# A feed-forward's down product with the weights held still and the activations moving

## The reference

```python
gate_scores = xf @ gate_w.T                 # two experts, top 1
one_hot = one_hot(argmax(softmax(gate_scores)), 2)
masked = xf[None] * one_hot.T[:, :, None]
h = relu(einsum('end,edh->enh', masked, w1) + b1[:, None, :])
expert_out = einsum('enh,ehd->end', h, w2) + b2[:, None, :]
shared = relu(xf @ sw1 + sb1) @ sw2 + sb2
out = expert_out.sum(axis=0) + shared       # then x = layernorm(x + out)
```

## Time and profile before

| | |
|---|---|
| Median of 3 runs | 635.62 us (633.32 to 635.85) |
| Profiled execution, its own time | 635.56 us |
| Its span, first to last instruction | 633.7 us (1.86 us lie around it) |
| `feed_forward0` on PE | 206.08 to 299.09 us |
| Mean granted clock of PE | 0.955 of full speed |

### The profile page before, as it was taken

How to read it: one execution, slowest core, us unless ns; L and a number is a source line. 1 busy time by engine, 2 the same in 40 slices (tenths; PEclk the granted TensorE clock), 3 DMA queues, 4 the chain that set the end, 5 groups by cost and what they waited for, 6 DMA issues and landing times.

```text
span 633.7 us, 11896 instructions
## 1 busy us (share of the span) xinstructions
PE 576.3 (91%) x4428; PEld 447.1 (71%) x4428; DVE 404.8 (64%) x1057; ACT 266.4 (42%) x531; POOL 226.7 (36%) x327
## 2 busy tenths in 40 slices
PE   3899999999987799999789999999889999999994
PEld 3657667766756599899556666665558888888883
DVE  2477877787764733554657788877246666666655
ACT  3586755575630322220055555555632222222220
POOL 2264545554320535363735555554510000000000
PEclk9699999999978999999959999999869999999999
DMA  5953131223000600002221221220000000000000
GB/s 208 324 197 122 69 134 67 102 100 125 10 1 0 252 1 1 1 2 68 70 74 49 63 63 48 68 73 4 4 1 0 2 1 18 1 18 2 1 18 17
DMA packets 25352, 37.64 MB, mean 59 GB/s; under 512 B 3536, under 2 KB 15568, under 8 KB 24912
## 3 DMA queue, kind: packets, MB, share of 16 engines
q1 hardware_dynamic: 25296, 36.89, 17.5%
HBM read 10.01 MB, written 1.05 MB: 17 GB/s over the span
## 4 chain that ended last, share of the span: by engine, by line
PE 63%; DVE 18%; issue 8%; ACT 3%; POOL 3%; DMA 2%; SPq 2%; POOLq 0%; DVEq 0%; ACTq 0%
PE f_O L1611 7%; PE f_O L801 6%; PE f_H L59 5%; PE f_H L61 5%; PE f_H L60 5%; PE a_MI L485 5%; DVE a_UA L366 4%; PE a_S L1328 4%; PE a_Y L437 4%; PE a_YP L1357 3%; PE a_S L1336 3%; PE a_PJ L59 2%; DVE a_m L1172 2%; PE a_S L423 2%; DVE a_rr L357 2%
## 5 line engine op out<-in xcount | busy, mean ns | idle before, releaser
L226 POOL TENSOR_TENSOR a_Y<-a_Y 128x256 f32<-128x256 f32 x64 | 59.5, 933 | 97.0 <-ACT a_Y L265 97.0
L366 DVE SCALAR_TENSOR_TENSOR a_UA<-a_UA,a_mask 128x768 f32<-128x768 f32 x64 | 68.3, 1075 | 27.1 <-ACT a_UA L273 26.6
L1172 DVE TENSOR_REDUCE a_m<-a_S 128x3 f32<-128x384 f32 x117 | 63.7, 554 | 31.6 <-PE a_S L1336 26.5
L1479 ACT ACTIVATE f_sg<-f_H 128x512 f32<-128x512 f32 x64 | 38.2, 597 | 103.1 <-PE f_H L61 103.1
L1557 DVE TENSOR_TENSOR f_hid<-f_H,f_sg 128x512 f32<-128x512 f32 x64 | 44.3, 692 | 53.2 <-PE f_H L61 43.1
L273 ACT ACTIVATE a_UA<-a_S,a_one 128x768 f32<-128x768 f32 x64 | 57.6, 900 | 44.8 <-PE a_S L424 44.6
L1096 POOL TENSOR_SCALAR_AFFINE_SELECT f_w<-f_w 128x256 f32<-128x256 f32 x128 | 51.8, 407 | 67.9 <-ACT f_w L1143 67.7
L1143 ACT ACTIVATE f_w<-a_ST 128x384 f32<-128x384 f32 x118 | 56.9, 493 | 39.7 <-PE a_ST L1334 39.7
L1611 PEld LDWEIGHTS f_O<-f_w,f_hid 128*128 128x128 f32 x512 | 65.9, 191 | 8.1 <-issue 3.3
L1611 PE MATMUL f_O<-f_w,f_hid 128*128 128x128 f32 x512 | 67.8, 276 | 2.0 <-DVE f_acc L1535 2.0
L437 PE MATMUL a_Y<-a_UA,a_V 128*64 128x256 f32 (+1 forms) x512 | 58.4, 351 | 0.0
(11 more groups left out here) (282 smaller groups left out, 1390.0 us busy)
## 6 DMA issues: line engine op xcount, KB each, us to landing
a_q<-a_c_h SPq DMA_DIRECT2D x16, 256.0 KB, 2.5
a_q<-a_c_l SPq DMA_DIRECT2D x16, 256.0 KB, 2.6
a_k<-a_c_h SPq DMA_DIRECT2D x16, 256.0 KB, 2.5
a_k<-a_c_l SPq DMA_DIRECT2D x16, 256.0 KB, 2.6
f_w<-in_f_w SPq DMA_DIRECT2D x1, 2048.0 KB, 8.8
a_q<-a_c_h SPq DMA_DIRECT2D x16, 128.0 KB
a_q<-a_c_l SPq DMA_DIRECT2D x16, 128.0 KB
a_k<-a_c_h SPq DMA_DIRECT2D x16, 128.0 KB
```

The source lines that it names most:

```text
L226: pool.tensor_tensor(Y2[:, v % 2, j, :], Y[:, v % 2, j, :], Y[:, v % 2, j, :], ALU.mult).then_inc(y2_ready, 1)
L366: dve.scalar_tensor_tensor(UA[:, j % 4, :, :], UA[:, j % 4, :, :], 1.0, mask[:, None, :].to_broadcast([P, 2, SW]), ALU.add, ALU.mult).then ...
L1172: dve.tensor_reduce(m3[:, b % 2, h % H1, :], s_bank(h)[:, 0:SW].rearrange("p (a n) -> p a n", a=3), AX.X, ALU.max).then_inc(max_done, 1)
```

## The change

Down now keeps a 128x128 chunk of w2 stationary and moves all 512 tokens of the block, so the result has features on partitions (`oT`) and must be turned back. Down of chunk n runs three steps (LAG) after its up, within the same block; the last three come after all up steps. Even chunks are one plain F32 product of 512 columns. For odd chunks DVE makes a high and a low F32R part with two instructions, and PE makes three F32R products. DVE writes max(h, -b) in place of relu(h + b); the difference is a constant vector w2'b, made once by PE (`cv_ready`) and added by ACT when it copies `O` to `oT` (`turn`). PE turns `oT` with four transposes into `T[1]`, and the residual reads it there. w2 is split by DVE at the start.

```diff
+    LAG = 3
-        hid = sb("f0_hid", [P, 2, NC, BT])
+        hid = sb("f0_hid", [P, 3, BT])
+        act_h, act_l = sb("f0_act_h", [P, 3, BT], F32R), sb("f0_act_l", [P, 3, BT], F32R)
+        w2_h, w2_l = sb("f0_w2_h", [P, NC, D], F32R), sb("f0_w2_l", [P, NC, D], F32R)
+        neg_b = sb("f0_negb", [P, NC])
...
         def _(act):
+            def turn(i):
+                act.wait_ge(d_ready, (i + 1) * NC)
+                if i >= 1:
+                    act.wait_ge(o_ready, i)
+                act.activation(oT[:, :], O[i % 2][:, :], ACT.Identity, bias=c_vec[:, 0:1]).then_inc(oT_ready, 1)
+
+            act.wait_ge(cv_ready, 1)
+            act.activation(c_vec[:, :], G[:, 64:65], ACT.Copy).then_inc(cv_read, 1)
+            act.wait_ge(cv_read, 1)
             for i in range(NBLK):
                 for c in range(0, NC, 2):
+                    n = i * NC + c
+                    if i >= 1 and c == 4:
+                        turn(i - 1)
+                    act.wait_ge(h_ready, n + 1)
+                    if n >= 6:
+                        act.wait_ge(d_ready, n - 5)
+                    act.activation(hid[:, n // 2 % 3, :], HP[n % 3][:, :], ACT.Relu, bias=b1[:, c:c + 1]).then_inc(h_act, 1)
...
             for t in range(2):
                 prep_high(act, mem, 1, t)
+            turn(NBLK - 1)
...
         def _(dve):
             dve.wait_ge(*before)
+            dve.tensor_scalar(neg_b[:, :], b1[:, :], -1.0, None, ALU.mult)
+            dve.tensor_copy(w2_h[:, :, :], w2[:, :, :]).then_inc(w2_split, 1)
+            dve.wait_ge(w2_split, 1)
+
+            def split_low(third):
+                cs = slice(4 * third, 4 * third + 4)
+                dve.tensor_tensor(w2_l[:, cs, :], w2[:, cs, :], w2_h[:, cs, :].bitcast(F32), ALU.subtract).then_inc(w2_split, 1)
...
-                dve.tensor_tensor(res[i % 2], O[i % 2][:, :].rearrange("p (t d) -> p t d", t=TB), xb[:, i % 2, :, :], ALU.add).then_inc(res_ready, 1)
+                dve.tensor_tensor(res[i % 2], T[1][:, :].rearrange("p (t d) -> p t d", t=TB), xb[:, i % 2, :, :], ALU.add).then_inc(res_ready, 1)
...
+            for i in range(NBLK):
                 for c in range(1, NC, 2):
+                    n = i * NC + c
+                    dve.wait_ge(h_ready, n + 1)
+                    if n >= 6:
+                        dve.wait_ge(d_ready, n - 5)
+                    high, low = act_h[:, n // 2 % 3, :], act_l[:, n // 2 % 3, :]
+                    dve.tensor_scalar(high, HP[n % 3][:, :], neg_b[:, c:c + 1], None, ALU.max).then_inc(high_step, 1)
+                    dve.wait_ge(high_step, n // 2 + 1)
+                    dve.scalar_tensor_tensor(low, HP[n % 3][:, :], neg_b[:, c:c + 1], high.bitcast(F32), ALU.max, ALU.subtract).then_inc(h_dve, 1)
+                    if i == 0 and c < 6:
+                        split_low(c // 2)
                     if i + 1 < NBLK and c in (3, 9):
                         prepare(i + 1, (c - 3) // 6)
...
-                    if c == 1 and i >= 2:
-                        residual(i - 2)
-                    if c == 7 and i >= 2:
+                    if c == 3 and i >= 2:
                         finish(i - 2)
+                    if c == 7 and i >= 1:
+                        residual(i - 1)
+            finish(NBLK - 2)
             residual(NBLK - 1)
             finish(NBLK - 1)
...
                     pe.wait_ge(xl_ready, 2 * i)
+                    if i >= 2:
+                        pe.wait_ge(res_ready, i - 1)
                     gate_transpose_x0(pe, mem, i, T[1])
...
+            def down(n):
+                i, c = divmod(n, NC)
+                if c == 0 and i >= 2:
+                    pe.wait_ge(oT_ready, i - 1)
+                out, start, stop = O[i % 2][:, :], c == 0, c == NC - 1
+                if c % 2 == 0:
+                    pe.wait_ge(h_act, n // 2 + 1)
+                    k = pe.matmul(out, w2[:, c, :], hid[:, n // 2 % 3, :], start=start, stop=stop)
+                else:
+                    pe.wait_ge(h_dve, n // 2 + 1)
+                    if i == 0 and c % 4 == 1:
+                        pe.wait_ge(w2_split, c // 4 + 2)
+                    high, low = act_h[:, n // 2 % 3, :], act_l[:, n // 2 % 3, :]
+                    pe.matmul(out, w2_h[:, c, :], high, start=start, stop=False)
+                    pe.matmul(out, w2_l[:, c, :], high, start=False, stop=False)
+                    k = pe.matmul(out, w2_h[:, c, :], low, start=False, stop=stop)
+                k.then_inc(d_ready, 1)
+
+            def turn(i):
+                pe.wait_ge(oT_ready, i + 1)
+                if i >= NBLK - 2:
+                    pe.wait_ge(mem["rb_ready"], 1 if i == NBLK - 2 else 3)
+                for t in range(TB):
+                    k = pe.transpose(T[1][:, t * P:(t + 1) * P], oT[:, t * P:(t + 1) * P], mem["ident"][:, :])
+                k.then_inc(o_ready, 1)
+
+            for c in range(1, NC, 2):
+                k = pe.matmul(G[:, 64:65], w2[:, c, :], b1[:, c:c + 1], start=(c == 1), stop=(c == NC - 1))
+            k.then_inc(cv_ready, 1)
+            for i in range(NBLK):
                 for c in range(NC):
+                    up(i, c)
+                    if i * NC + c >= LAG:
+                        down(i * NC + c - LAG)
+                    if i >= 1 and c == 6:
+                        turn(i - 1)
...
+                                if k == 1:
+                                    pe.wait_ge(res_ready, NBLK - 1)
                             prep_project(pe, mem, b, k - 1, (T[1], G)[k - 1])
+            for n in range(NBLK * NC - LAG, NBLK * NC):
+                down(n)
+            turn(NBLK - 1)
```

More of the change, by code:

```diff
@@ L609, in feed_forward0 @@
                 parts[1][e] = sb(f"f0_x{name}1{e}", [P, BT], F32R)[:, :]
-        hid = sb("f0_hid", [P, 2, NC, BT])
+        hid = sb("f0_hid", [P, 3, BT])
+        act_h, act_l = sb("f0_act_h", [P, 3, BT], F32R), sb("f0_act_l", [P, 3, BT], F32R)
+        w2_h, w2_l = sb("f0_w2_h", [P, NC, D], F32R), sb("f0_w2_l", [P, NC, D], F32R)
+        neg_b = sb("f0_negb", [P, NC])
+        c_vec = sb("f0_cvec", [P, 1])
+        oT = sb("f0_oT", [P, BT])
         res = [mem["RES"][:, :, :, :].rearrange("p a b d -> p (a b) d"), mem["a1_wqk"][:, :].rearrange("p (t d) -> p t d", d=D)]
@@ L626, in feed_forward0 @@
         h_act, h_dve = sem("h_act"), sem("h_dve")
-        o_ready = sem("o_ready")
+        d_ready, oT_ready, o_ready = sem("d_ready"), sem("oT_ready"), sem("o_ready")
+        cv_ready, cv_read, w2_split, high_step = sem("cv_ready"), sem("cv_read"), sem("w2_split"), sem("high_step")
         res_ready, ln_step, var_ready, rstd_ready = (sem(n) for n in "res_ready ln_step var_ready rstd_ready".split())
@@ L741, in finish @@
                 norm_apply(dve, X[:, TB * i:TB * i + TB, :], res[i % 2], mv[:, i % 2], rstd, TB).then_inc(x_done, 1)
-            for i in range(NBLK + 1):
+            for i in range(NBLK):
                 for c in range(1, NC, 2):
-                    if i < NBLK:
-                        dve.wait_ge(h_ready, i * NC + c + 1)
-                        dve.tensor_scalar(hid[:, i % 2, c, :], HP[(i * NC + c) % 3][:, :], b1[:, c:c + 1], 0.0, ALU.add, ALU.max).then_inc(h_dve, 1)
+                    n = i * NC + c
[8 more added lines that the diff above has]
+                        split_low(c // 2)
                     if i + 1 < NBLK and c in (3, 9):
@@ L774, in prepare @@
                 elif part == 1:
+                    pe.wait_ge(cv_read, 1)
                     gate_scores(pe, mem, i, xT, G)
@@ L790, in up @@
                 three_pass(pe, HP[n % 3][:, :], w1_h[:, e, cols], w1_l[:, e, cols], xh[p][e], xl[p][e]).then_inc(h_ready, 1)
[L792 to L804, removed]
@@ L806, in _ @@
-            for i in range(NBLK + 1):
-                for c in range(NC):
[L808 to L811, removed]
+            def down(n):
[15 more added lines that the diff above has]
+                k.then_inc(d_ready, 1)
```

## The result

The changed kernel takes 641.62 us (median of 13 runs, 636.75 to 651.68). The kernel before took 633.32 us beside it (13 runs, 632.35 to 635.85). The ratio is 1.0094, with a 95% interval of 1.0070 to 1.0117: slower by 0.9%, some 6 us. The two medians lie 8.3 us apart, more than the ratio says, because the ratio leaves out the slow run of 651.68 us, and because the runs of each kernel form two groups, where the median falls into the lower one before (632.4 to 633.4) and into the upper one after (641.6 to 643.1). A second measurement of the same kernel gave 1.0103 (1.0084 to 1.0123). The forecast was 642.8 us and slower.

The account below looks back on a forecast made before the run. The prediction took PE to set the pace except in block 0, where it waits for DVE. Block changes and the end chain put the next stage 7.2 us later: 635.56 + 7.2 = 642.8 us, range 638.0 to 647.0.

Parts of the forecast that it names:

- Block 0: First feed-forward block: DVE's extra start-up work and two-instruction odd chunks delay PE; block 1 starts 7.5 us later.
- Block 1: Second block: PE's ups, downs, transposes and scores plus one residual wait, 20.35 us against 20.86, 0.5 us less.
- Block 2: Third block: waits for bank 5 and the residual after the expert choice, 22.15 us against 22.19.
- Block 3 to the last rotation of batch 0: Last block up to chunk 5's rotation: cheaper downs but a longer DVE bank, 12.15 us against 11.98.
- From there to the second high part of batch 1: POOL, ACT, SP and DMA chain at the stage's end, untouched by the change: 19.75 us, holding ACT's last turn.
- From there to the next stage: After the chain: ACT's copy 0.69, PE's transposes 0.9, DVE's sum 0.69 and hand-overs 0.1 us.
- Odd and even chunks: Down products on PE: odd chunks 0.70 us and even ones 0.87, against 0.89 for a down step before.
- rival A: Down on PE: weight loads set the pace, an even chunk costs 0.53 us, time 637.8 us; chance 0.13.
- Rival C: Block 0: POOL keeps DVE's cast of w2 out until 217.08, bank 1 3.9 us later, 646.7 us; chance 0.12.
- The wait of 0.3 us for the turned residual: Block 1: PE comes at 15.05 us but the turned residual leaves its buffer only at 15.3.
- Rival B: Stage's end: batch 0's chain does not hold the last turn, as POOL or DMAs come sooner, 635.3 us; chance 0.05.
- Rival D: Next stage: starts slower on PE's cold clock, about +1 us, 643.8 us; its chance counted within the forecast's 0.70.

Follow-up runs that it names:

- the fillers: Changed kernel plus twenty one-pass products, whose sums nobody reads, in PE's block 0 wait: 641.47 us, ratio to before 1.0108.
- w2_split_on_pool: Changed kernel with POOL instead of DVE splitting w2 in block 0, DVE only making -b: 646.16 us, ratio to before 1.0142.
- pool_waits: Changed kernel with POOL's two differences of block 0 waiting for DVE's cast of w2: 638.59 us, ratio to before 1.0073.
- turn_first: Changed kernel with ACT's last turn moved ahead of the two high parts of batch 1: 636.02 us, ratio to before 1.0019.
- chain_early: Changed kernel with last turn first, batch 0's high parts one step earlier on ACT, POOL's two sums between its weight pieces: 634.35 us, ratio 0.9993.
- before_pool_waits: Kernel before the change, with POOL's two differences of block 0 waiting for the previous stage's last normalisation: 638.86 us, ratio to before 1.0049.
- again: The changed kernel, unaltered, run a second time beside the kernel before: 641.73 us, ratio to before 1.0103.

## Why the prediction was right, point by point

The chain of reasons held, and its sum was 1.8 us too long for the stage. Against the 93.01 us of before it gave 100.2, and 98.36 were measured. That 642.8 lies only 1.2 us from the median 641.62 is partly luck: the sum starts from an execution of 635.56 us, 2.2 above the median of the kernel before beside it, and the difference of 7.2 us is what ought to be compared, with 5.35 for the stage and some 6 for the time. One caution for reading starts: an up product that follows a plain chunk has a record that begins 0.40 us early (L59 at 228.86 lasts 0.80, and L60 comes 0.64 later for the usual 0.23). So block 1 really began at 229.26. Block starts 1 to 3 are all shifted alike. The terms, from the stage's start at 206.20 (206.08 before):

| Term | Predicted, us | Measured, us |
|---|---|---|
| Block 0 | 23.37 | 23.06 |
| Block 1 | 20.35 | 20.11 |
| Block 2 | 22.15 | 21.74 |
| Block 3 to the last rotation of batch 0 | 12.15 | 12.05 |
| From there to the second high part of batch 1 | 19.75 | 18.87 |
| From there to the next stage | 2.40 | 2.53 |
| Stage | 100.17 | 98.36 |

*Odd and even chunks.* An even chunk takes 0.86 us (0.87 predicted, 0.53 in rival A), an odd one 0.70 as predicted. The 0.87 has luck in it. The 0.13 us for 128 columns in the earlier trace rows are 2.5 clocks a column at 2.4 GHz, and the prediction took two; with 2.5 an even chunk would have come out near 1.07. Measured are 0.857 us for 1024 columns, two clocks each. Rival A is refuted: loads fell and time did not. PEld went from 78.30 to 61.73 us over the stage, and a down chunk of two loads is as long as the eight-load step of before within 0.04 us. The Trainium skill (Trainium Kernel Development and Optimization, Performance Expectations) takes weight-load busy time, beside the share of peak arithmetic, as the measure of how near PE is to its limit. The trace does not bear out the weight-load part here: PEld's share of the stage fell from 84% to 63%, and PE was busy for 86 us as before. A plain record of 512 moved columns takes 0.43 us and a one-pass one 0.23, each with one weight load.

*Block 0.* The bias products took 1.36 us and were hidden, as assumed, since PE had to wait for DVE anyway. DVE's order came as worked out, bank 1 at 214.43 for 214.7 and up 8 at 222.82 for 223.05. What the prediction did not see is PE's low clock after the wait of 2.58 us. By the fillers it costs 0.5 us. That the block still came out 0.3 us shorter than the sum is luck: other terms were too long by more. Rival C did not happen: the cast ran at once in 0.95 us, and it was POOL that waited, L663 (L656 before) taking 1.26 us for 0.45. Its price was also wrong: a cast that starts at 217.08 ends at 218.1, not at 217.1, so bank 1 would come 4.9 us later, and the time would be 647.7, above the stated range. The Trainium skill (SBUF — State Buffer, Who interferes with whom) says that who issues first keeps the shared ports for its whole instruction. L663, which ends 0.3 us after the cast, agrees with such a lock. L336 in w2_split_on_pool does not show the order: its first instruction starts 0.47 us before POOL's L659 and yet lasts 3.67 us, through L659, L660 and L527. In the kernel before, too, it was the first instruction of L336 that was held (3.05 us), not the second as the prediction read. That the block's delay reaches the end undiminished is shown by experiment: w2_split_on_pool lengthens it by 2.2 us and the stage by 2.2, pool_waits shortens both by 1.6.

*Blocks 1 and 2.* Block 1 is PE's own work: busy 20.09 of 20.11 us. The wait of 0.3 us for the turned residual was not there. Block 2 has the predicted waits, but smaller: 0.93 us for bank 5 (1.3 predicted), 0.43 before the transposes of the masked x (0.7).

```profile
264.05 0.50 PE L59 MATMUL f_H<-f_xh,w_h 128*128 128x512 f32 x1 [0.93 <-DVE f_act_l L780]
...
266.13 0.63 PE L584 MATMUL f_T<-ident,w 128*128 128x128 f32 x4 [0.43 <-issue]
```

*The end.* This was the core of the forecast, and turn_first and chain_early show it: the turn stands behind a chain of POOL, ACT, SP and the DMAs that the change makes late but does not touch. In the kernel before, 48 down products covered that chain; the change took the cover away. Rival B is out, as the chain did hold the turn. Its length was the largest error, 18.87 us for 19.75. POOL's part is the same (9.48 us from the rotation to SP's first issue, 9.53 before), and so is the landing of the last DMA (1.9 to 2.0 us after SP's last issue). The difference lies mostly in SP's issues, whose first pair took 1.98 us in the earlier trace rows and 1.23 here. One issue of the eight, the second, lasted 1.34 us where the others last 0.6; the other profile of that code, before_pool_waits, has one too, the sixth with 1.28, and none of the profiles of the changed kernel and its versions has one. Why is open. By the prediction's own terms PE would have stood for 7.9 us (from 296.6 to 304.5) and not for its 7; 7.07 were measured because this chain was shorter.

*The rest of the kernel.* Rival D, a dearer start of `attention1` on the low clock, is there and does not last. The granted clock of its first 5 us is 0.50 for 1.00 before, and the fifth row maximum of DVE starts 6.8 us into the stage for 5.5. At the nineteenth the two kernels are level, 19.10 us for 19.16, as the prediction had it for the first 15 us. The first row is of the kernel before, the second of the changed one:

```profile
318.25 1.01 DVE L1172 TENSOR_REDUCE a_m<-a_ST 128x3 f32<-128x384 f32 x2
323.66 1.01 DVE L1232 TENSOR_REDUCE a_m<-a_ST 128x3 f32<-128x384 f32 x2
```

So the 1.4 us that the profiled execution of the changed kernel lost after the stage were lost later than that. The same kernel in again was 2.4 us shorter than before after the stage, so nothing of this is put down to the change. The stage's +5.35 us and the ratio's 4.4 to 7.4 us agree without it. The predicted +7.2 lies at the upper end of that.

## What to carry to other kernels

Before work is moved away from the end of a stage, look at what runs beside it on the other queues: this change removed PE's 48 trailing products and left a four-queue chain as the bound that had been free by only 2 us, with the turn of the last block queued behind it. A new instruction at the end of an in-order queue inherits every wait ahead of it: putting it ahead of two others was worth 4.6 us of a stage that had grown by 5.4, and 3.1 us once the next stage was under way. A stage's end that is marked on one engine can hide what another still owes. An engine with slack over a stage can still set the time of its first microseconds. DVE's second read of each bank and the split of w2 hurt mostly there: with one plain product instead of the three faster ones the stage was 3.1 us shorter, and 2.2 shorter where the chain was out of the way.

## What the runs showed of the hardware

DVE was kept waiting through a whole row of POOL instructions, not through one: L336 takes 0.65 us for two beside nothing but POOL's small memsets (0.30 us each), 3.49 with POOL's differences beside it, and 5.01 when a split of w2 follows them without a gap. POOL's long memsets do it as well: four maskings take 3.97 us through two of them. They did not hold DVE's subtraction for the low part of w2, which took 0.68 us beside one (at 216.42 in the changed kernel) and 1.73 beside POOL's differences. DVE's reads of PSUM banks (L778, L780) took 0.75 us whatever POOL did. A wait that takes POOL away from one DVE instruction moves the collision to another, and in before_pool_waits to a dearer one.

The granted clock of PE after a pause did not repeat between executions: after pauses of 1.44 and 1.46 us in the same code it fell in one and stayed in the other, 1.5 us of difference in block 0. Nor did it go by the length of the pause: in the kernel before it stayed at 1.00 after 2.90 us, and in the changed kernel it fell to 0.50 after 2.58. Runs of one kernel differed by some 4 us in what follows the stage. At 1.2 GHz a one-pass product of 512 columns took 0.43 us for 0.23, and four transposes 1.12 for 0.66 (records, with their modelled ends).
